# Turning attention probabilities with VectorE blocks and SBUF copies in a cross-attention and FFN kernel

## What is computed

```python
q = rope(layernorm(x) @ wq); k = rope(ctx @ wk); v = ctx @ wv
attn = softmax(q @ k.T / sqrt(128) + mask)          # 32 heads, 256 x 256 each
x = x + (attn @ v) @ wo
w = lut4[bits of qweight]                           # mask of the reference picks the 4 bit table
x = x + layernorm(x) @ w.T + bias
```

## Time and profile before

| | us |
|---|---|
| median of 3 runs | 2459.45 |
| lowest, highest | 2458.3, 2460.17 |
| the profiled execution: time | 2458.84 |
| the profiled execution: span from first to last instruction | 2457.1 |
| TensorE, VectorE, ScalarE, GpSimd busy | 2448.4, 1503.9, 1135.7, 451.3 |

### The profile page before, as it was taken

The page is one execution under the profiler, slowest core; times in us unless marked ns, Lnnn a source line. Parts: engine busy times, 40 slices in busy tenths (PEclk is TensorE's granted clock), DMA queues, the critical chain, the costliest instruction groups (busy, mean ns, idle before and its releaser), DMA issues.

```text
span 2457.1 us, 35798 instructions
## 1 busy us (share of the span) xinstructions
PE 2448.4 (100%) x12990; PEld 2108.6 (86%) x12990; DVE 1503.9 (61%) x3558; ACT 1135.7 (46%) x2475; POOL 451.3 (18%) x674
## 2 busy tenths in 40 slices
PE   9999999999999999999999999999999999999999
PEld 8999998888888888888888888888888888888887
DVE  7887776555656555556565555565565655565553
ACT  5555434464545455545554444444444444443110
POOL 1000001222222222222222222222222222222211
PEclk9999999999999999999999999999999999999999
DMA  7466566322222222222245412212121211214211
GB/s 255 157 211 195 186 221 226 119 66 86 69 78 78 76 88 66 82 69 78 73 151 184 146 61 67 72 61 69 52 74 60 61 61 61 69 60 160 89 69 52
DMA packets 178030, 255.36 MB, mean 104 GB/s; under 512 B 15552, under 2 KB 114112, under 8 KB 177856
## 3 DMA queue, kind: packets, MB, share of 16 engines
q1 hardware_dynamic: 177856, 253.08, 31.3%
HBM read 181.73 MB, written 71.30 MB: 103 GB/s over the span
## 4 chain that ended last, share of the span: by engine, by line
PE 97%; DVE 1%; DMA 1%; ACT 0%; issue 0%; SPq 0%; ACTq 0%; DVEq 0%
PE bank L751 29%; PE bank L828 28%; PE bank L767 7%; PE bank L873 7%; PE bank L800 7%; PE bank L713 7%; PE bank L690 6%; PE bank L788 5%; PE bank L662 1%; DMA ln_row<-in_L_xattn_wk 0%; DVE residual L1426 0%; PE bank L671 0%; PE bank L651 0%; PE bank L778 0%; DMA k_scratch<-small_split 0%
## 5 line engine op out<-in xcount | busy, mean ns | idle before, releaser
L751 PE MATMUL bank<-acts_split,weights_split 128*128 128x512 f32 (+1 forms) x3168 | 767.9, 391 | 0.0
L828 PE MATMUL bank<-weights_split,small_split 128*128 128x512 f32 x3072 | 740.9, 390 | 0.3 <-DVE small_split L1639 0.3
L828 PEld LDWEIGHTS bank<-weights_split,small_split 128*128 128x128 f32 x3072 | 574.5, 188 | 119.3 <-DVE small_split L1639 0.5
L751 PEld LDWEIGHTS bank<-acts_split,weights_split 128*128 128x128 f32 x3168 | 564.7, 188 | 104.3
L1762 POOL TENSOR_SCALAR probs<-probs,row_numbers 128x256 f32<-128x256 f32 x512 | 239.4, 480 | 1329.3 <-DVE row_numbers L1629 1329.3
L1618 DVE CUSTOM_DVE_ANT_0 probs<-bank,mask_tile 128x256 f32<-128x256 f32 x512 | 197.0, 421 | 262.1 <-PE bank L767 247.3
L1149 ACT ACTIVATE probs<-probs,row_numbers 128x256 f32<-128x256 f32 x512 | 256.6, 502 | 46.1 <-DVE row_numbers L1624 42.2
L1165 ACT ACTIVATE small_split<-bank 128x512 fp32r<-128x512 f32 x127 | 75.9, 598 | 417.5 <-PE bank L800 417.4
L1755 POOL TENSOR_TENSOR rope_x<-rope_x,sin_t 128x512 f32<-128x512 f32 (+1 forms) x132 | 166.6, 1262 | 486.2 <-ACT rope_x L1132 485.5
L1589 DVE SCALAR_TENSOR_TENSOR rope_a<-bank,cos_t 128x512 f32<-128x512 f32 (+1 forms) x132 | 89.1, 675 | 262.7 <-ACT rope_x L1132 262.7
L767 PEld LDWEIGHTS bank<-small_split 128*128 128x128 f32 x1536 | 217.9, 190 | 20.7 <-issue 0.8
(11 more groups left out here) (117 smaller groups left out, 2375.3 us busy)
## 6 DMA issues: line engine op xcount, KB each, us to landing
raw<-in_L_xattn_wq SPq DMA_DIRECT2D x61, 512.0 KB, 4.5
raw<-in_L_xattn_wo SPq DMA_DIRECT2D x60, 512.0 KB, 3.5
k_scratch<-small_split SPq DMA_DIRECT2D x64, 256.0 KB, 2.3
v_scratch<-small_split SPq DMA_DIRECT2D x32, 512.0 KB, 2.9
x_scratch<-raw SPq DMA_DIRECT2D x64, 256.0 KB, 2.8
acts_split<-x_scratch SPq DMA_DIRECT2D x32, 512.0 KB, 6.4
mask_tile<-in_mask_BxSxS_ff SPq DMA_DIRECT2D x64, 256.0 KB, 3.6
small_split<-k_scratch SPq DMA_DIRECT2D x64, 256.0 KB, 2.6
```

Source lines behind the costliest of these rows:

```text
L751: last = pe.matmul(query_bank(j)[:, 0:wide], wq_s[:, h, c, a, :], xT[:, c, m, b * S:b * S + wide], start=c == 0 and i == 0, stop=c == C - ...
L828: last = pe.matmul(out_ps[part][:, :], o_s[:, a, u % 2 * S + t * P:u % 2 * S + (t + 1) * P], wo_s[:, h, m, n * BANK:(n + 1) * BANK], start ...
```

## The change

For 252 of the 256 units the probabilities are no longer turned by TensorE. Units 1, 253, 254 and 255 (`PE_TURNS`) keep `turn`. For the others `add_mask` writes the probabilities with keys spread over four groups (key m*4+b at column b*128 + t*64 + m), `exponent` and `normalize` work on that layout, VectorE turns the tile's 32 x 32 blocks in place (`turn_blocks`), and SyncE issues four copies from SBUF to SBUF (`move_blocks`), each taking 32 partitions of 2 KB rows to 128 partitions of 512 B rows, into the low half of the split tile. `turned_high` and `turned_low` then read that half in place of PSUM. `turned_high` and `turned_low` of an odd unit u-1 come after `exponent(u)` and `invert(u)` in step u; those of an even unit u-1 after `query_swap` and `query_add`. The order of queries in the turned tile follows blocks of 32, so the residual rows are read from a copy of x in that order (`x_rows`), and the output rows are put back in order on the host. `scores`, `query` and `project` keep their instructions; `attend` reads runs of 32 columns.

```diff
     AHEAD, LAG = 2, 3
+    PE_TURNS = (1, NU - 3, NU - 2, NU - 1)
+    QUAD = 32
+
+    def landed(u):
+
+        return sum(v not in PE_TURNS for v in range(u % 2, u + 1, 2))
+
+    def blocks(u):
+
+        return sum(v not in PE_TURNS for v in range(u + 1))
...
+        prob_rows = prob_t[:, :].rearrange("p (s n) -> p s n", s=2)
+        prob_blocks = prob_t[:, :].rearrange("p (s b t m) -> p s t m b", s=2, b=P // QUAD, t=TS)
+        prob_parts = prob_t[:, :].rearrange("p (s b t m) -> p s t b m", s=2, b=P // QUAD, t=TS)
...
+            def move_blocks(u):
+
+                sp.wait_ge(p_blocks, blocks(u))
+                sp.wait_ge(o_mm, 1 + u // 2)
+                for a in range(P // QUAD):
+                    done = sp.dma_start(pT_moved[:, LO, u % 2, a, :].bitcast(F32),
+                                        prob_rows[a * QUAD:(a + 1) * QUAD, u % 2, :])
+                    done.then_inc(pT_in[u % 2], 16)
+
             for u in range(NU):
                 if u % REP == 1:
                     load_values(u - 1)
                 if u % REP == REP - 1 and u + 1 < NU:
                     load_keys(u + 1)
                     load_mask(u + 1)
+                if u % 2 and u not in PE_TURNS:
+                    move_blocks(u)
...
                 if u in SIDE:
                     store_row(*SIDE[u])
+                if u % 2 == 0 and u not in PE_TURNS:
+                    move_blocks(u)
                 if u % REP == REP - 1 and u in PIECE:
                     load_weights(u)
                 if u % REP != REP - 2 and u + 1 in PIECE:
...
             for u in range(NU):
                 scores(u)
-                if u - 1 in SIDE:
-                    pe.wait_ge(x_lo, 2 * SIDE[u - 1][0] + SIDE[u - 1][1] + 1)
-                if u >= AHEAD:
+                if u - 1 in PE_TURNS:
                     turn(u - 1)
                 for j, chunks in WORK.get(u, ()):
-                    if u == 1:
-                        query(j, chunks[:C // 2])
-                        turn(u - 1)
-                        query(j, chunks[C // 2:])
-                    else:
-                        query(j, chunks)
+                    query(j, chunks)
                 if u in SIDE:
-                    turn_side(*SIDE[u], u)
+                    turn_side(*SIDE[u])
...
             def turned_high(u):
                 act.wait_ge(o_mm, 1 + u // 2)
-                if u == 0:
-                    act.wait_ge(k_stored[0], 16 + 16 * (NB * K_SLOT0 + 1))
-                    act.wait_ge(v_stored, 16 + 16 * (NB * len(V_TURNS) - 3))
-                act.wait_ge(pT_tr, 2 + u + 1)
-                act.activation(pT_s[:, HI, :, u % 2 * S:(u % 2 + 1) * S],
-                               pT_ps[:, :].rearrange("p (k n) -> p k n", k=TS), ACT.Copy).then_inc(pT_hi, 1)
+                if u in PE_TURNS:
+                    act.wait_ge(pT_tr, PE_TURNS.index(u) + 1)
+                    source = pT_ps[:, :]
+                else:
+                    act.wait_ge(pT_in[u % 2], 4 * 16 * landed(u))
+                    source = pT_s[:, LO, u % 2, :].bitcast(F32)
+                act.activation(pT_s[:, HI, u % 2, :], source, ACT.Copy).then_inc(pT_hi, 1)
...
-                if u == AHEAD:
+                if u - 1 in PE_TURNS:
                     turned_high(u - 1)
                 if u - 1 in DONE:
                     query_high(DONE[u - 1])
-                if u < AHEAD:
-                    exponent(u)
-                if u >= 1 and u != AHEAD:
+                exponent(u)
+                if u % 2 == 0 and u and u - 1 not in PE_TURNS:
                     turned_high(u - 1)
-                if u >= AHEAD:
-                    exponent(u)
                 if u in DONE and u not in LATE:
                     query_swap(DONE[u])
+                if u % 2 and u - 1 not in PE_TURNS:
+                    turned_high(u - 1)
...
                 for t in range(TS):
                     last = dve.tensor_tensor_reduce(
-                        out=probs[:, u % 2, t, :], in0=s_ps[:, t * S:(t + 1) * S],
-                        in1=mask_t[:, t, :], scale=1.0, scalar=-3.0e38, op0=ALU.add, op1=ALU.max,
+                        out=probs[:, u % 2, t, :] if u in PE_TURNS else prob_blocks[:, u % 2, t],
+                        in0=by_keys(u, s_ps[:, t * S:(t + 1) * S]),
+                        in1=by_keys(u, mask_t[:, t, :]), scale=1.0, scalar=-3.0e38, op0=ALU.add, op1=ALU.max,
...
+            def turn_blocks(u):
+                dve.wait_ge(p_ready, u + 1)
+                dve.transpose(prob_rows[:, u % 2, :], prob_rows[:, u % 2, :]).then_inc(p_blocks, 1)
+
             def turned_low(u):
-                half_of = slice(u % 2 * S, (u % 2 + 1) * S)
+                source = pT_ps[:, :] if u in PE_TURNS else pT_s[:, LO, u % 2, :].bitcast(F32)
                 dve.wait_ge(pT_hi, u + 1)
-                dve.tensor_tensor(pT_s[:, LO, :, half_of], pT_ps[:, :].rearrange("p (k n) -> p k n", k=TS),
-                                  pT_s[:, HI, :, half_of].bitcast(F32), ALU.subtract).then_inc(pT_lo, 1)
+                dve.tensor_tensor(pT_s[:, LO, u % 2, :], source, pT_s[:, HI, u % 2, :].bitcast(F32),
+                                  ALU.subtract).then_inc(pT_lo, 1)
...
+                if u % 2 == 0 and u and u - 1 not in PE_TURNS:
                     turned_low(u - 1)
-                    output_weights_lo(3)
+                if u not in PE_TURNS:
+                    turn_blocks(u)
                 if u in DONE and u not in LATE:
                     query_cos(DONE[u])
                 if u in SIDE:
                     x_low(*SIDE[u], pT_ps)
                 if u in DONE and u not in LATE:
                     query_add(DONE[u])
+                if u % 2 and u - 1 not in PE_TURNS:
+                    turned_low(u - 1)
```

More of the change, by code:

```diff
@@ L12, in wait, with build_xattn_ffn @@
         self.eng.wait_ge(self.sem, self.base + self.n - but)
-def build_xattn_ffn(nc, x, ctx, mask, wq, wk, wv, wo, qweight, lut4, bias, rope_cos, rope_sin, out):
+def build_xattn_ffn(nc, x, ctx, mask, wq, wk, wv, wo, qweight, lut4, bias, x_rows, rope_cos, rope_sin, out):
     from contextlib import ExitStack
@@ L187, in build_xattn_ffn @@
         v_s = R[:, 3584:4096].rearrange("p (k l n) -> p k l n", k=TS, l=2)
-        pT_s = R[:, 4608:6656].rearrange("p (l k n) -> p l k n", l=2, k=TS)
+        pT_s = R[:, 4608:6656].rearrange("p (l u n) -> p l u n", l=2, u=2)
+        pT_keys = R[:, 4608:6656].rearrange("p (l q k j) -> p l k q j", l=2, k=TS, j=QUAD)
+        pT_moved = R[:, 4608:6656].rearrange("p (l u a n) -> p l u a n", l=2, u=2, a=P // QUAD)
         w4_s = W[:, :].rearrange("p (c l n) -> p c l n", c=C, l=2)
@@ L281, in build_xattn_ffn @@
         p_ready, pT_tr, pT_hi, pT_lo = sem("p_ready"), sem("pT_tr"), sem("pT_hi"), sem("pT_lo")
+        p_blocks, pT_in = sem("p_blocks"), [sem(f"pT_in{s}") for s in range(2)]
         o_mm, o_hi, o_lo = sem("o_mm"), sem("o_hi"), sem("o_lo")
@@ L308, in v_turn, with prob_part @@
             return b * len(V_TURNS) - 1 + V_TURNS[i]
+        def prob_part(u, t):
+            return probs[:, u % 2, t, :] if u in PE_TURNS else prob_parts[:, u % 2, t]
         def fold(view, units):
@@ L770, in scores, with turn_side @@
                 last.then_inc(s_mm, 1)
-            def turn_side(e, j, u):
+            def turn_side(e, j):
                 if j == 0:
                     pe.wait_ge(row_ok, e + 1)
-                pe.wait_ge(pT_lo, 1 + u)
+                pe.wait_ge(x_lo, 2 * e + j)
                 for c in range(4):
@@ L785, in turn @@
                 pe.wait_ge(pT_lo, u + 1)
+                if u > 1:
+                    pe.wait_ge(x_lo, 2 * NT)
                 for t in range(TS):
                     for k in range(TS):
-                        last = pe.transpose(pT_ps[:, k * S + t * P:k * S + (t + 1) * P],
-                                            probs[:, u % 2, t, k * P:(k + 1) * P], ident[:, :])
+                        last = pe.transpose(pT_cols[:, t, k], probs[:, u % 2, t, k * P:(k + 1) * P], ident[:, :])
                 last.then_inc(pT_tr, 1)
@@ L799, in attend @@
                     for i, (a, m) in enumerate(PASSES):
-                        last = pe.matmul(o_ps[:, :], v_s[:, k, a, :], pT_s[:, m, k, :],
+                        last = pe.matmul(o_ps[:, :], v_s[:, k, a, :], pT_keys[:, m, k],
                                          start=k == 0 and i == 0, stop=k == TS - 1 and i == 2)
@@ L810, in attend_one @@
                     for i, (a, m) in enumerate(PASSES):
-                        last = pe.matmul(o_ps[:, half_of], v_s[:, k, a, :], pT_s[:, m, k, half_of],
+                        last = pe.matmul(o_ps[:, half_of], v_s[:, k, a, :], pT_keys[:, m, k, u % 2 * (S // QUAD):(u % 2 + 1) * (S // QUAD)],
                                          start=k == 0 and i == 0, stop=k == TS - 1 and i == 2)
@@ L1148, in exponent @@
                 for t in range(TS):
```

(22 more changed lines are left out.)

13 lines of the change are left out of this document (8 added, 5 removed).

## The result

The changed kernel takes 2554.56 us (median of 4 runs, 2552.78 to 2556.14), the kernel before 2459.78 us on the same chip: a ratio of 1.0386 [1.0368, 1.0404]. The profiled execution took 2554.64 us with a span of 2552.9 us, 95.8 us more than before's 2457.1. The forecast was 2471 us with a range of 2418 to 2515. The direction was right; the time lies 84 us above the forecast and above the range.

What follows compares the result with a forecast made beforehand. TensorE, busy 2448.4 of 2457.1 us, was taken to bound the kernel. From 2458.8 us, 116 came off for removed turns and waits of 79, 21, 13 and 15 were added: 2471 us, range 2418 to 2515.

Steps and rivals of the forecast that it cites:

- the load of step 16g+3 behind four copies: On SP's queue the weight load waits for the block turn and four copies, going out 4.8 us later, at 7.2 us.
- The clock: Rival: after each 5.3 us wait TensorE runs 4 us at 1.2 GHz, losing 30 us, so 2501 us; chance 0.12.
- The removal: On TensorE, 252 turns dropped at 0.46 us each take 116 us off the time.
- The wait of step 16g+4: TensorE idles 5.3 us before `attend` in rounds 1 to 15, 79 us in all.
- the end of the block turn: VectorE finishes the turn of unit 16g+3 at 5.55 us into the step at best, releasing the copies.
- The small waits: TensorE waits 21 us in steps 16g+3, 13 us in 16g+2 and 15 us in 16g+11 and 16g+15.
- The mask instructions: On VectorE, `add_mask` writing 512 bytes apart costs 0.23 us more an instruction, 0.46 us a unit.
- The copies: 252 x 256 KB of copies land in 2.6 us each and stay covered, without much to spare.
- a load that isn't behind the copies: Side figure within the cheap rival: with the load not behind the copies, waits total 49 us, giving 2392 us.
- the signs named ahead: Load issued 7 to 9 us into steps 16g+3, idle 4 to 6 us before `attend` in 16g+4, slower masks, 0.68 us transpose.
- a cheap mask and early load: Rival: masks cost nothing more and the load lands in 3.5 us, waits total 75 us, 2418 us; chance 0.26.
- The block turn in two ticks: Rival: VectorE's block turn takes 1.23 us, two ticks an element, 2550 us or so; chance 0.08 shared with no effect.

Runs made afterwards that it cites:

- e1: The changed kernel with SP issuing the weight load of steps 16g+3 ahead of that unit's four copies: 2461.76 us.
- e2: The changed kernel with 56 unused transposes of the identity on TensorE before `attend` in steps 16g+4 of rounds 1 to 15: 2533.55 us.
- e4: The kernel before without TensorE's turns of 251 units, so the output isn't attention's: 2351.39 us.
- e10: The kernel before with all turns kept and `attend` reading its moving operand in runs of 32 columns: 2467.65 us.
- e12: e1 with the weight loads of steps 16g, 16g+7, 16g+9, 16g+11 and 16g+13 also issued ahead of the copies: 2451.35 us.
- e6: The changed kernel with 38 unused transposes of the identity on TensorE before `attend` in steps 16g+4: 2538.12 us.
- e3: The changed kernel with `add_mask` writing its elements side by side, so the output isn't attention's: 2521.14 us.

## Why the prediction was wrong in size and right in direction

The mechanism that decides, and its place, were forecast: the load of step 16g+3 behind four copies, its wait before `attend` in steps 16g+4, and lesser ones before `project`. e1 shows its price: 93 of the 95 us. Point by point:

1. **The clock: the step that failed.** The sum put a wait of 79 us in, and nothing for what follows it; the fall of the clock stood among the rivals, with a chance of 0.12, as though it could come or not beside a wait that I took as certain. It follows from that wait (e2). Its size was right: 30 us forecast for it, 31 us by the steps, 30 by TensorE's busy time. It is the largest single part of the 84 us, and a term that the sum put at nothing. The Trainium skill, TensorE: Matmul & The Clock Gate, section "Why this matters for your kernels", warns of long gaps between bursts; here the trace agrees, with 0.50 behind 5.3 us of idle time. I had written that the trace before couldn't test it and let that decide against it.
2. **The removal was priced too high by 15 us.** A turn is worth 0.433 us, not 0.46 (e4: 7 us in all). And the layout that the copies leave makes `attend` read in runs of 32 columns, 7.6 us (e10). The forecast weighed the new layout on VectorE and ScalarE, but not on TensorE.
3. **The wait of step 16g+4** was 85 us, not 79 (5.7 a round, not 5.3). The forecast was inconsistent here: it took 5.55 us "at best" for the end of the block turn although its own next paragraph has VectorE 1.9 us late in this very step. The turn ended 7.27 us into the step, the copies' issue took 2.49 us, not 1.6, and the load went out at 9.84 us, not 7.2. Most of it was cancelled because step 16g+3 itself grew to 7.70 us: the masks began 7.96 us into step 16g+4 where 7.5 were forecast.
4. **The small waits** were 2 us (16g+3), 1 us (16g+2) and 8 us (16g+11, 16g+15) more than forecast. The mask instructions came cheaper than forecast (611 ns, not 650) and the block turn slightly dearer (712 ns, not 680); but `normalize`, taken as a tenth dearer at most, takes 93 ns more an instruction, a fifth, or 0.19 us a unit on the way to the block turn.
5. **Unforeseen:** 6.8 us in step 2, where unit 1's turn on TensorE now waits 5.0 us for VectorE; 9.5 us scattered over other steps; 4 us outside the loop.
6. **The copies** are covered, as forecast. ScalarE waited for them 12.5 us in all, 22 times.

Together 31 (clock) + 15 (removal) + 6 + 11 (waits) + 7 + 9 + 4 = 83 of the 84 us. The same lack shows in the prediction's own figure for a load that isn't behind the copies, 2392 us: e1 tested it and gave 2462. There the waits were put at 49 us, and the steps of e1 show 95, of them 21 in steps 16g+4, where the figure has none. Of the signs named ahead, all came but two: the load was issued 9.8 us into the step, not 7 to 9, and one of the fifteen waits was 6.6 us, over the 4 to 6.

The direction has some luck in it. The forecast was 12 us slower, and the parts above that it had wrong are larger than that; they all went the same way. The range was wrong because it was built from these cases as alternatives: with forecast and clock as one case the likeliest time would have been 2501 us and its own range some 2480 to 2520. That would not have held 2554.6 either: the other terms, each too low, make the rest.

The rivals: a cheap mask and early load lost, as the mask's price lay near the forecast and the load was later, not earlier. The block turn in two ticks is excluded by 712 ns, though its total of 2550 is close to what came. The Trainium skill, Vector Engine (DVE) Microarchitecture Reference, section 3.8, says that the block transpose sustains one element a cycle, and this trace agrees: 712 ns for 512 elements, beside 680 ns for a plain pass of that size. By an estimate from section 5.2 of the same page of the Trainium skill the two masks should have cost 0.34 to 0.74 us more a unit; measured are 0.38.

Not tried: loads ahead of the copies in step 16g+3 with the turn of step 2 also left to VectorE, and a queue of their own for the copies. Of the 9.5 us in other steps, 5.9 stand in steps 16g+9 and 16g+13, which e12's loads end; the rest is open.

## What to carry to other kernels

When a change puts a waiting issue into a queue, follow the next load behind it to its last user: here one line's place on SP was worth 93 us and the whole verdict, against 101 us that the change took off TensorE. Where a forecast holds a long wait of TensorE, price the slower clock behind it in the same term, not as a rival. And an operation moved to another engine costs what that engine's slack costs in each step: the 30 units in crowded steps were better left where they were, by 41 us.

## What was not expected of the hardware

- Behind an idle 5.3 us the granted clock was 0.50 in the next 2.7 us and 0.67 in the 5 us after; turns with the identity in the gap held it at 1.00 (e2). In e6, with 38 of them and a rest of idle time behind, it fell in rounds 2, 5 and 12 (2.0 and twice 2.5 us idle) and held in the others (1.3 to 1.8 us).
- A mask pass that writes each element 512 bytes from the last takes 611 ns for 256 elements, 420 with neighbouring ones (e3).
- Six matmuls of 512 columns take 0.06 us longer when the moving operand comes in runs of 32 columns (e10).
- GpSimd's multiplication of 128x256 takes 573 ns in runs of 64 elements; before, in runs of 256, 480. No run changes this alone.
